# A language-model tower on one core: where the inverse roots of the latent stage's head norms are computed

## The reference

```python
def rmsnorm(x, w, eps=1e-06):
    rms = lax.rsqrt(mean(x * x, axis=-1, keepdims=True) + eps)
    return w * (x * rms)
...
latent = silu(x_norm @ w_comp)
q, k, v = split(latent @ w_qkv, 3, axis=-1)          # 12 heads of 16 each
q = rope(rmsnorm(q, qn_w))
k = rope(rmsnorm(k, kn_w))
q_f = elu(q) + 1.0
k_f = elu(k) + 1.0
```

## Time and profile before

| | |
|---|---|
| time, median of 3 runs | 2994.08 us (2992.48 to 2994.65) |
| time of the profiled execution | 2991.19 us |
| its span, first to last instruction | 2989.4 us |
| latent stage, loop and its two ends | 1042.2 to 1743.0 us of the span, 700.8 us |
| powers of the head norms on POOL | 32, 133.0 us busy |
| mean granted clock of TensorE | 0.709 |

### The profile page before, as it was taken

The page is one execution under the profiler, slowest core; times in us unless marked ns, Lnnn a source line. Parts: engine busy times, 40 slices in busy tenths (PEclk is TensorE's granted clock), DMA queues, the critical chain, the costliest instruction groups (busy, mean ns, idle before and its releaser), DMA issues.

```text
span 2989.4 us, 34363 instructions
## 1 busy us (share of the span) xinstructions
PE 1876.6 (63%) x11766; PEld 1375.2 (46%) x11766; DVE 1243.5 (42%) x3630; ACT 1017.4 (34%) x2621; POOL 420.4 (14%) x330
## 2 busy tenths in 40 slices
PE   0175546668787556566656666767676129999960
PEld 0032115546565444455445555555555016666640
DVE  4868877743444444544454423333333300000003
ACT  0266786422222234333433322223232013333310
POOL 5101110000000022212222200000000340000026
PEclk9955555556666577787778767676766559999985
DMA  2000000140000000000000000000000214333323
GB/s 60 0 0 0 0 0 1 40 132 0 0 0 0 0 1 0 0 0 0 0 0 0 1 1 0 0 0 0 0 0 1 67 62 111 111 108 106 106 75 103
DMA packets 97749, 81.13 MB, mean 27 GB/s; under 512 B 23624, under 2 KB 90216, under 8 KB 97704
## 3 DMA queue, kind: packets, MB, share of 16 engines
q1 hardware_dynamic: 90024, 64.83, 8.0%
q0 software_dynamic: 7680, 15.74, 1.8%
HBM read 53.02 MB, written 27.53 MB: 27 GB/s over the span
## 4 chain that ended last, share of the span: by engine, by line
issue 35%; PE 34%; DVE 14%; ACT 8%; POOL 7%; SPq 1%; DVEq 1%; DMA 0%; POOLq 0%; ACTq 0%
PE bank L2076 8%; PE bank L928 7%; PE bank L2087 6%; ACT bank L686 4%; POOL WK L1453 4%; PE bank L921 3%; POOL R L2006 2%; POOL WK L968 2%; PE bank L902 2%; PE bank L1133 1%; ACT WK L703 1%; PE bank L536 1%; PE bank L1553 1%; PE bank L1519 1%; PE bank L2064 1%
## 5 line engine op out<-in xcount | busy, mean ns | idle before, releaser
L928 PE MATMUL bank<-WK,R 96*128 96x256 f32 (+2 forms) x1280 | 363.0, 445 | 4.0 <-ACT WK L913 4.0
L902 PE MATMUL bank<-ident,WK 128*96 128x128 f32 x448 | 110.4, 398 | 314.6 <-DVE WK L951 120.9
L928 PEld LDWEIGHTS bank<-WK,R 96*128 96x128 f32 (+2 forms) x1280 | 266.1, 214 | 85.2 <-issue 35.3
L968 POOL TENSOR_TENSOR WK<-WK,mhalf 128x2 f32<-128x2 f32 (+1 forms) x96 | 78.0, 813 | 1415.0 <-DVE WK L945 757.4
L2076 PE MATMUL bank<-R 96*128 96x512 f32 x552 | 255.3, 598 | 1.6 <-ACT R L2105 1.6
L1976 DVE TENSOR_TENSOR WK<-bank,WK 128x192 f32<-128x192 f32 x92 | 26.5, 351 | 503.5 <-PE bank L2087 503.5
L902 PEld LDWEIGHTS bank<-ident,WK 128*96 128x96 f32 x448 | 70.5, 181 | 347.9 <-DVE WK L951 134.4
L921 PE MATMUL bank<-R,WK 96*128 96x192 f32 x640 | 193.6, 470 | 33.8 <-ACT WK L909 32.7
L2087 PEld LDWEIGHTS bank<-R 128*128 128x128 f32 x1104 | 182.9, 190 | 33.5 <-issue 33.5
L2087 PE MATMUL bank<-R 128*128 128x192 f32 x1104 | 194.6, 326 | 0.0
L2112 ACT ACTIVATE R<-bank,WK 128x512 f32<-128x512 f32 x138 | 94.9, 688 | 291.2 <-PE bank L2076 291.2
(11 more groups left out here) (428 smaller groups left out, 3627.3 us busy)
## 6 DMA issues: line engine op xcount, KB each, us to landing
R<-in_L_ffn_w SPq DMA_DIRECT2D x46, 576.0 KB
moe_rows_in<-zeros SPq DMA_DIRECT2D x1, 8832.0 KB, 29.9
R<-moe_rows_in SPq DMA_DIRECT2D x23, 384.0 KB
moe_rows_out<-WK SPq DMA_DIRECT2D x23, 384.0 KB, 4.1
out<-R SPq DMA_DIRECT2D x4, 768.0 KB, 4.0
WK<-in_L_ffn_b SPq DMA_DIRECT2D x23, 96.0 KB
R<-in_L_attn_w SPq DMA_DIRECT2D x3, 384.0 KB, 6.4
moe_rows_in<-R,WK POOLq DMA_INDIRECT x64
```

The lines of the kernel that those rows point to most:

```text
L902: mm = nc.tensor.transpose(a.bank[b][0:C, c * NM + i * P:c * NM + (i + 1) * P], src[:, i, c * C:(c + 1) * C], ident[:, :])
L928: mm = nc.tensor.matmul(out, w[0:C, c, m], a.xT[0:C, c, :], start=(c == 0), stop=(c == 1))
L968: nc.gpsimd.tensor_tensor(a.rs[:, 0:n], a.ve[:, 0:n], mhalf[:, 0:n], ALU.pow).then_inc(f.root, 1)
```

## The change

The power on POOL (L1453) and the two waits for it on DVE go. In their place DVE computes the roots of both tiles at once, 48 values per partition, right behind L1352: a first guess from the bits (shift right by one, subtract from 0x5f3759df), half of the argument with its sign turned, and four Newton steps of three instructions each. Each of the 15 instructions is followed by a wait for its own end. L1352 gets such a wait too. A work area `a.hw` of 96 values per partition is added to each stream, which moves some later small tiles of a stream from one region of on-chip memory (`WK`) to the other (`R`) or back. The counts of `f.root` and `f.var` are three per block in place of five.

```diff
+            a.hw = take(48 * M)
...
+        def inverse_roots(ch, y, x, half, t):
+
+            ch.step(nc.vector.tensor_scalar(y.bitcast(I32), x.bitcast(I32), 1, None, ALU.arith_shift_right))
+            ch.step(nc.vector.tensor_scalar(y.bitcast(I32), y.bitcast(I32), -1, 0x5f3759df, ALU.mult, ALU.add))
+            ch.step(nc.vector.tensor_scalar(half, x, -0.5, None, ALU.mult))
+            for _ in range(4):
+                ch.step(nc.vector.tensor_tensor(t, y, y, ALU.mult))
+                ch.step(nc.vector.tensor_tensor(t, t, half, ALU.mult))
+                ch.step(nc.vector.scalar_tensor_tensor(out=y, in0=t, scalar=1.5, in1=y, op0=ALU.add, op1=ALU.mult))
...
-                nc.vector.tensor_scalar(ve, ve, 1.0 / DH, 1e-6, ALU.mult, ALU.add).then_inc(f.var, 1)
+                ch.step(nc.vector.tensor_scalar(ve, ve, 1.0 / DH, 1e-6, ALU.mult, ALU.add))
+            inverse_roots(ch, a.rs[:, 0:24 * M], a.ve[:, 0:24 * M], a.hw[:, 0:24 * M], a.hw[:, 24 * M:48 * M])
...
-            v.wait_ge(f.var, per(g, 5, 3))
...
-                v.wait_ge(f.root, per(g, 5, 2 + i))
...
-            for i in range(M):
-                pool.wait_ge(f.var, per(g, 5, 2 + i))
-                w = slice(24 * i, 24 * i + 24)
-                nc.gpsimd.tensor_tensor(a.rs[:, w], a.ve[:, w], mhalf[:, w], ALU.pow).then_inc(f.root, 1)
```

More of the change, by code:

```diff
@@ L1341, in vector_l_1 @@
             yield
-            v.wait_ge(f.root, per(g, 5, 1))
+            v.wait_ge(f.root, per(g, 3, 1))
             twice_normed(v, ch, g, a, f, f.xr)
@@ L1419, in vector_l_2 @@
             yield
-            v.wait_ge(f.root, per(g, 5, 4))
+            v.wait_ge(f.root, per(g, 3, 2))
             v.wait_ge(f.proj_p, per(g, 1, 1))
@@ L1431, in vector_l_2 @@
             yield
-            v.wait_ge(f.root, per(g, 5, 5))
+            v.wait_ge(f.root, per(g, 3, 3))
             for i in range(M):
@@ L1446, in pool_l_1 @@
         def pool_l_1(pool, g, a, f):
-            roots(pool, a, f, per(g, 5, 1), 2 * M)
+            roots(pool, a, f, per(g, 3, 1), 2 * M)
             for _ in range(4):
                 yield
-            for i in range(M):
-                pool.wait_ge(f.var, per(g, 5, 2 + i))
-                w = slice(24 * i, 24 * i + 24)
-                nc.gpsimd.tensor_tensor(a.rs[:, w], a.ve[:, w], mhalf[:, w], ALU.pow).then_inc(f.root, 1)
             for _ in range(3):
@@ L1459, in pool_l_2 @@
                 yield
-            roots(pool, a, f, per(g, 5, 4))
+            roots(pool, a, f, per(g, 3, 2))
             yield
             yield
-            roots(pool, a, f, per(g, 5, 5))
+            roots(pool, a, f, per(g, 3, 3))
             for _ in range(3):
```

## The result

The changed kernel takes **3028.3 us** (median of 4 runs, 3025.4 to 3034.6) and the kernel before, run beside it, 2994.4 us (4 runs, 2992.5 to 2995.1): a ratio of **1.0117, interval 1.010 to 1.0135**. It is slower, 33.9 us by the medians, where 29.7 were forecast. The profiled execution took 3029.9 us. All medians here leave out launches in a slower state of the chip (one of the kernel both, at 3263.6 us and a granted clock of 0.63).

What follows compares the result with a forecast made beforehand. It took a chain between engines as the bound, with DVE waiting for POOL's powers and PE for DVE. Seven A (16.2), seven B (11.3) and the end blocks gave 29.7 us more: 3023.8 us, range 3012 to 3034.

Steps and rivals of the forecast that it cites:

- The price of a link: DVE's fifteen dependent instructions, at 0.22 to 0.25 us each, were to add 3.58 us per block.
- The waits behind L1363: New waits behind the second sum of squares on DVE (L1352 before the change) were to add 0.24 us per block.
- Half turn A, with ACT in the way: Half of each loop turn: ACT's table load and back-to-back exponentials delay L1392 by 2.32 us; DVE alone would give 2.14.
- Half turn B: Other half of each loop turn: DVE arrives 3.82 us later, finds 2.21 of slack, so L1392 moves by 1.61.
- First and last block: Blocks at the stage's ends: 3.82 us added less slack of 2.6 and 2.7, giving +1.2 and +1.1.
- Does it all reach the end?: PE behind L1392: the delay counts in full, and 2 us more of waiting costs no second time through the clock.
- the clock: Rival, chance 0.04: longer PE waits lower the granted clock elsewhere or delay its return; 28 us on top, 3052 us.
- sign of being wrong: Links under 0.2 us or integer ones several times as long; turn +7.6 us; or stage grows with PE's clock lower.
- Absorbed: Rival, chance 0.04: DVE's own waits for PE behind L1392 absorb the delay; no change, 2994 us.
- the whole chain is paid: Rival, chance 0.05: POOL's waits cover something ending as late, so 16 x 3.82 = 61 us come on top; 3055 us.
- Short links: Rival, chance 0.03: DVE's links cost only 0.09 us each, 1.59 per block; some 6 us faster, 2988 us.
- DVE is freed: Rival, chance 0.02: without POOL's reads DVE's neighbouring work shrinks, 3 us back per block; some 18 us faster, 2976 us.

Runs made afterwards that it cites:

- both: Kernel before, POOL's powers kept and used, with the 15 links added on DVE and their result unused; 3021.5 us, ratio 1.0125 to the kernel before.
- no_roots: Changed kernel without any inverse roots, heads scaled by the mean square itself; 2963.7 us, ratio 0.9915 to the kernel before.
- woven: Changed kernel with two Newton steps, independent instructions between links, sums and mean squares of both tiles in one instruction each; 2985.0 us, ratio 0.9974 to before.
- two_steps: Changed kernel with two Newton steps in place of four; 2991.0 us, ratio 1.0004 to the kernel before.
- full_before: Kernel before with 96 unused transposes per block filling PE's wait; 2983.6 us, ratio 0.9948 to the kernel before.
- full_after: Changed kernel with 116 unused transposes per block filling PE's wait; 2990.1 us, ratio 0.9993 to the kernel before.
- woven_four: Changed kernel, four Newton steps kept, independent instructions between links, sums and mean squares of both tiles in one instruction each; 2991.3 us, ratio 0.9995 to before.
- full_woven: The kernel woven with 92 unused transposes per block filling PE's wait; 2952.5 us, ratio 0.9847 to the kernel before.

## Why the prediction was right

- **The wait names what bounds.** Held. What was taken from POOL did not come back as such: DVE's 31.2 us of waits for powers are gone, and no_roots shows that they were worth 26.8 us of path.
- **The price of a link.** 3.58 forecast, 3.57 measured. The nearest row, a TENSOR_TENSOR of the same shape at 0.208, gave it: the new L1323 takes 0.208 too. The integer links, left to the range, take 0.188, and the next link starts 0.22 behind each. The table of the Trainium skill (VectorE: DVE Perf Modes, TRN2 errata), by which the change would have left the time nearly alone, is out by a factor of two here, as its own warning says.
- **The waits behind L1363.** 0.24 forecast. From the first sum to the first rotary instruction it was 1.36 us and is 5.26, so the addition is 3.90 in A and 0.33 of it is these waits; in B it is 3.83.
- **Half turn A, with ACT in the way.** +2.32 forecast, 14.89 - 12.45 = +2.44. 0.09 of the 0.12 is the larger wait at L1363, since nothing on the way to the exponentials had slack. DVE alone would have given 2.14 by the forecast's own terms; the exponentials stand back to back.
- **Half turn B.** +1.61 forecast, 12.94 - 11.38 = +1.56.
- **First and last block.** +1.2 and +1.1 forecast, 12.20 - 10.99 = +1.21 and 12.83 - 11.71 = +1.12.
- **The sum.** 29.7 forecast, 30.3 measured on the path.
- **Does it all reach the end?** Yes, and this is the term that was off: the step "2 us more of waiting shouldn't cost a second time" put the clock's change at nothing, and the stretch grew by 7.1 us more than the path, the medians by 3.6 more than the path. A turn grew by 4.6 us where 3.9 were forecast. The mechanism is the one given as a rival, *the clock*, at a quarter of its price or less: 6.3 of the 7.1 us are PE's longer busy time for the same matmuls in windows outside the path. It was argued from one place, PE at 0.50 behind its longest wait, and there it is right: the twelve transposes behind that wait take 2.8 us, the low level, before and after. But the level at other places of the turn, at L902 and L1499 for one, now differs from turn to turn. By the forecast's own sign of being wrong, "the turn's PE work shows a lower clock", the profile after is divided: 0.74 to 0.77 in five of seven turns and 0.81 in two, in place of 0.78. So this sign was met in part, and the other two were not.
- **The rivals.** *Absorbed* and *the whole chain is paid* fall by the path. *Short links* falls by the 0.24. *DVE is freed* falls by the kernel both.

That the total came out within 4.5 us of the forecast owes something to the clock's term being small in this kernel. In others of this study what the path leaves unexplained was as large as the path's own change, or nearly: 13.2 of woven's 15.6 us were taken back, and two_steps got 7.2 against a path 7.1 longer.

**What stays open.** Why the turns settle where they do. 85.3 us is the turn of before, of woven, of most turns of full_before, and of full_after, and the mean of two_steps' and woven_four's three turns; their paths in a turn differ by up to 5.7 us. PE's busy time moves the right way in each (53.5 us of a turn in woven, 52.8 in before, 50.1 to 50.8 in two_steps), but for woven it makes up 0.7 of the 1.7 us by which its path in a turn is shorter. The rows don't show what ties a turn to that length, and I have no experiment that does. For the changed kernel the remainder is placed above, all but 0.8 us. For woven, full_woven shows what the clock can give back, 5.8 us in each of its two turns at 0.98; that all of woven's remainder is the clock is argued, not shown.

## What to carry to other kernels

Ask of a step that is moved off a slow engine what the path gets back, which is the waiting engine's slack and not the slow engine's busy time; here 1.7 us a block of POOL's 8.3, less than half of what fifteen links in a chain cost. Price a chain by link, and before adding one look for independent instructions to stand between its links: that took a link from 0.22 to 0.24 us down to 0.10 to 0.12. And where PE waits long and works in bursts, don't take its clock as given: compare turn with turn, and measure an edit once with the wait filled to its end, and look whether the full level is held in every turn: where it was, path and time agreed.

## What the hardware did that I had not expected

- **The same code ahead of the stage took 1014.2 to 1036.3 us.** The kernels have the same program up to the stage. Windows of the part from 900 us to the memset of L979, in before, two_steps and full_after:

```profile
900.00:1025.40 125.40, 95.58 (x366) 72.84 (x366) 49.11 (x198) 30.23 (x97) 3.13 (x4) 0.58 0.00 0
```

```profile
900.00:1036.32 136.32, 108.19 (x366) 80.20 (x366) 49.75 (x199) 30.80 (x99) 3.14 (x4) 0.51 0.00 0
```

```profile
900.00:1014.18 114.18, 82.53 (x366) 65.05 (x366) 48.97 (x196) 30.34 (x97) 3.14 (x4) 0.66 0.00 0
```

  The same 366 matmuls, with granted clocks of 0.58, 0.51 and 0.66. Runs of the kernel before fall into groups (near 2981, 2986, 2991 and 3001), and an edit can't be blamed for which one a profile falls in. A change of 5 us is read from the stretch that it touches.
- **A filler that ends 3 to 4 us early keeps the level one time and loses it another** (3.22 us of idle, then 1.53 for twelve transposes; 4.06, then 2.18 for nine). One that ends 0.8 us early, in full_after, kept it in six turns of seven alike. But full_before's kept it in every half turn A (0.61 us of idle, then 1.53 for twelve) and lost it in five of eight half turns B (in one, 1.43 us of idle, 0.64 for the four transposes of L902, and then 2.74 for twelve). A gap of 3.22 us kept the level and one of 1.43 did not, so the gap alone does not decide.
- **Work on DVE's path was lengthened at no cost in time**, and shortened at little gain: two_steps' path is 7.1 us longer than before's in an equal stretch, woven's 15.6 shorter in one 2.4 shorter.
